# Four output blocks and four with tanh chunks of three and five; VectorE's loop end two instructions later; two tails reordered

## What is computed

```python
x = x + attention(x, mask, Wq, Wk, Wv, Wo)        # 8 batches, 512 x 1024
# then a scan over 512 time steps, carry q, p of shape (8, 1024):
def derivative(q, p, drive, coupling, bias):
    dq = q - q ** 3 / 3.0 - p + drive + jnp.tanh(q) @ coupling.T + bias
    dp = EPSILON * (q + ALPHA - BETA * p)
    return dq, dp
# classical Runge-Kutta: four derivatives a step, each at the state that
# the one before gives; then q and p are clipped to +-20
x = x + scan(rk4_step, (cond, cond), x)            # the trace of q
```

## Time and profile before

| | |
|---|---|
| median of 3 runs | 5646.72 us (5643.98 to 5647.08) |
| the profiled execution | 5647.13 us, its span 5645.3 us |
| VectorE busy | 5124.9 us, 91% of the span |
| TensorE busy, matmuls | 4394.8 us, 78% |
| ScalarE busy | 2677.3 us, 47% |
| granted TensorE clock, mean | 0.995 |
| chain that ended last | VectorE 48%, TensorE 35%, issue 13%, ScalarE 3% |

### The profile page before, as it was taken

How to read it: one execution, slowest core, us unless ns; L and a number is a source line. 1 busy time by engine, 2 the same in 40 slices (tenths; PEclk the granted TensorE clock), 3 DMA queues, 4 the chain that set the end, 5 groups by cost and what they waited for, 6 DMA issues and landing times.

```text
span 5645.3 us, 584273 instructions
## 1 busy us (share of the span) xinstructions
PE 4394.8 (78%) x263627; PEld 3697.3 (65%) x263627; DVE 5124.9 (91%) x31055; ACT 2677.3 (47%) x12552; POOL 5.7 (0%) x16
## 2 busy tenths in 40 slices
PE   7887777777777777777777777777777777777777
PEld 3436666666666666666666666666666666666666
DVE  5569999999999999999999999999999999999999
ACT  3334444444444444444444444444444444444444
POOL 0000000000000000000000000000000000000000
PEclk9999999999999999999999999999999999999999
DMA  5100000000000000000000000000000000000000
GB/s 221 47 16 0 0 7 0 7 0 0 7 0 7 0 7 0 7 0 0 7 0 7 0 7 0 0 7 0 7 0 7 0 0 7 0 7 0 7 0 7
DMA packets 11597, 57.06 MB, mean 10 GB/s; under 512 B 2616, under 2 KB 2616, under 8 KB 8512
## 3 DMA queue, kind: packets, MB, share of 16 engines
q1 hardware_dynamic: 11056, 55.84, 2.5%
q10 hardware_dynamic: 528, 1.05, 0.1%
HBM read 40.11 MB, written 16.78 MB: 10 GB/s over the span
## 4 chain that ended last, share of the span: by engine, by line
DVE 48%; PE 35%; issue 13%; ACT 3%; DVEq 0%; DMA 0%; SPq 0%; ACTq 0%
PE ps L634 30%; DVE xb L675 23%; DVE tanh_parts L675 7%; DVE xb L835 6%; ACT xb L444 3%; DVE xb L855 2%; DVE drive L675 2%; DVE xb L963 2%; DVE xb L952 2%; PE ps L523 2%; DVE xb L959 1%; DVE xb L913 1%; PE ps L541 1%; PE ps L578 1%; PE ps L557 1%
## 5 line engine op out<-in xcount | busy, mean ns | idle before, releaser
L634 PE MATMUL ps<-coup,tanh_parts 128*16 128x96 f16 (+1 forms) x262272 | 4047.0, 220 | 1171.7 <-DVE tanh_parts L675 877.6
L634 PEld LDWEIGHTS ps<-coup,tanh_parts 128*16 128x16 f16 x262272 | 3536.9, 89 | 1682.4 <-DVE tanh_parts L675 1197.8
L675 DVE SCALAR_TENSOR_TENSOR xb<-xb 128x64 f32<-128x64 f32 (+2 forms) x17413 | 3006.7, 210 | 110.5 <-issue 75.3
L444 ACT ACTIVATE xb<-xb 128x24 f32<-128x24 f32 (+1 forms) x4098 | 940.7, 230 | 2352.3 <-DVE xb L675 2276.4
L835 DVE STREAM_TRANSPOSE xb<-ps 128x96 f32<-128x96 f32 (+1 forms) x4096 | 1285.6, 314 | 38.8 <-PE ps L634 0.6
L675 DVE SCALAR_TENSOR_TENSOR tanh_parts<-xb,tanh_parts 128x24 f16<-128x24 f32 (+1 forms) x4098 | 704.3, 172 | 192.0 <-ACT xb L444 169.9
L493 ACT ACTIVATE xb<-xb 128x64 f32<-128x64 f32 x2048 | 499.6, 244 | 64.2
L450 ACT ACTIVATE tanh_parts<-xb 128x24 f16<-128x24 f32 (+1 forms) x2050 | 470.8, 230 | 64.6
L855 DVE SCALAR_TENSOR_TENSOR xb<-xb 128x64 f32<-128x64 f32 x2049 | 451.2, 220 | 0.0
L462 ACT ACTIVATE tanh_parts<-xb 128x24 f16<-128x24 f32 (+1 forms) x2048 | 356.8, 221 | 121.0
L456 ACT ACTIVATE xb<-xb 128x64 f32<-128x64 f32 x1024 | 262.6, 256 | 95.5 <-DVE xb L675 95.4
(11 more groups left out here) (69 smaller groups left out, 715.3 us busy)
## 6 DMA issues: line engine op xcount, KB each, us to landing
xb<-in_x SPq DMA_DIRECT2D x8, 2048.0 KB, 8.1
drive<-in_x_pt SPq DMA_DIRECT2D x8, 2048.0 KB, 24.5
out_pt<-drive SPq DMA_DIRECT2D x16, 1024.0 KB, 4.7
drive<-in_coupling_t SPq DMA_DIRECT2D x8, 512.0 KB, 11.6
mask_v<-in_cond SPq DMA_DIRECT2D x8, 132.0 KB
probs<-in_wo ACTq DMA_DIRECT2D x1, 1024.0 KB, 5.6
w_qkv<-in_wq SPq DMA_DIRECT2D x1, 64.0 KB, 3.7
w_qkv<-in_wk SPq DMA_DIRECT2D x1, 64.0 KB, 5.3
```

What stands on the lines that cost most here:

```text
L444: nc.scalar.activation(cols(tanh_sb, CHUNKS[j]), cols(q, CHUNKS[j]), ACT.Tanh, scale=unit_of[1.0])\
L634: last = nc.tensor.matmul(product(s, j)[SQ * g:SQ * g + ROWS, :], tanh_parts[:, s % 2, k, :], coup[:, k, part, g, n0:n1, :].rearrange("p c ...
L675: return V.scalar_tensor_tensor(out=out, in0=a, scalar=factor, in1=c, op0=ALU.mult, op1=op1)
```

## The change

`SUMS = [(0, 4), (4, 8)]` divides the outputs, in TensorE's columns, in PSUM and in the two turns. `CHUNKS` goes on dividing tanh, q 0, q 1 and the rests. On VectorE, `forecast_third` and `with_first_part` of stage 0 move from its tail into `until_rest`, so that the loop's end stands behind them. `q_sum_g0` moves from the tail of stage 3 to between q 1 and rest 1 of stage 0. `drive_step_of` moves from the tail of stage 0 to that of stage 3. Within the tails, `cubic_of(1)` goes ahead of `p_sum_g0`, and `z_of_first` ahead of `g0_of`.

```diff
 CHUNKS = [(0, 3), (3, 8)]
 NCH = len(CHUNKS)
+SUMS = [(0, 4), (4, 8)]
...
         def product(stage, j):
-            w = CHUNKS[j][1] - CHUNKS[j][0]
+            w = SUMS[j][1] - SUMS[j][0]
             return ps[:, NCH * (stage % 2) + j, 0:w * SQ]
+        def turned_rows(j):
+            return turned_sums[:, SUMS[j][0]:SUMS[j][1], :].rearrange("p c r -> p (c r)")
...
             def products(s, kj, j, begins, ends):
-                n0, n1 = CHUNKS[j]
+                n0, n1 = SUMS[j]
                 for k in range(*CHUNKS[kj]):
...
-                V.transpose(turned_sums[:, CHUNKS[j][0]:CHUNKS[j][1], :].rearrange("p c r -> p (c r)"),
-                            product(s, j)).then_inc(product_turned[j], 1)
+                V.transpose(turned_rows(j), product(s, j)).then_inc(product_turned[j], 1)
...
                 if s == 0:
                     y_less_g0()
+                    q_sum_g0()
...
                 rest_of(parity, 1, made)
-                return made
-
-            def after_rest(s, now_at, made):
-
                 if s == 0:
+
                     forecast_third(made)
                     with_first_part(1, z_first_part, z2, made)
+                return made
+
+            def after_rest(s, now_at, made):
+
+                if s == 0:
+                    cubic_of(1, made)
                     p_sum_g0()
-                    cubic_of(1, made)
-                    drive_step_of(now_at)
                     base_of(1, made)
...
                 if s == 3:
-                    g0_of(made - 1)
+                    dve.wait_ge(side_ready, made - 1)
                     z_of_first()
+                    g0_of()
                     with_first_part(0, z_first_part, z, made)
                     cubic_of(0, made)
-                    q_sum_g0()
+                    drive_step_of(1 - now_at)
                     base_of(0, made)
```

More of the change, by code:

```diff
@@ L922, in forecast_first, with g0_of @@
                 axpy(forecast[:, :], less_q[:, :], 1 / 3, q_st[3][:, :]).then_inc(forecast_ready, 1)
-            def g0_of(now):
-                dve.wait_ge(side_ready, now)
+            def g0_of():
                 axpy(g0[:, :], p_st[:, :], -BETA, q_st[0][:, :])
@@ L979, in _ @@
             for j in range(NCH):
-                last = V.transpose(turned_sums[:, CHUNKS[j][0]:CHUNKS[j][1], :].rearrange("p c r -> p (c r)"),
-                                   product(1, j))
+                last = V.transpose(turned_rows(j), product(1, j))
             last.then_inc(start_turned, 1)
@@ L988, in _ @@
             dve.wait_ge(setup, 11)
-            q_sum_g0()
+            drive_step_of(0)
             def until_rest(s, now_at, now):
@@ L1027, in until_rest @@
                 rest_of(parity, 1, made)
+                if s == 0:
+                    forecast_third(made)
+                    with_first_part(1, z_first_part, z2, made)
                 return made
@@ L1032, in after_rest @@
                 if s == 0:
-                    forecast_third(made)
-                    with_first_part(1, z_first_part, z2, made)
+                    cubic_of(1, made)
                     p_sum_g0()
-                    cubic_of(1, made)
-                    drive_step_of(now_at)
                     base_of(1, made)
```

## The result

The changed kernel takes 5701.91 us (median of 4 runs, 5699.95 to 5705.17) against 5646.9 before (4 runs): ratio 1.0099, 95% interval 1.0081 to 1.0116. It is slower, by 55 us. The forecast was 5706, range 5655 to 5750. The profiled execution has a span of 5700.3 us (before 5645.3) at the same mean granted clock, 0.995.

A forecast was written before the change was run, and what follows sets the result against it. The prediction took a ring of waits, not one engine's work, to bound the kernel. Terms -0.17 + 0.08 + 2 x 0.18 - 4 x 0.01 = +0.23 us a pass, +59 us on 5647.1: 5706, range 5655 to 5750.

The forecast's parts named there:

- The third piece on TensorE: On TensorE: matmul groups take 0.056 us; stage 3's first transpose is held 0.14 longer plus 0.04, until 1.12.
- The turns: VectorE's transposes of 128 columns take 0.24 us start to start, 0.315 long, midway between 96 and 160 columns.
- My rival, that they cost what the 96-column turn does: VectorE's 128-column transposes cost what the 96-column one does: 72 to 143 us below the sum, some 5600; chance 0.09.
- that of the 160-column one: VectorE's 128-column transposes cost what the 160-column one does: +135 us, 5841; chance 0.06.
- The loop's end: VectorE's stage 1 behind the branch: two instructions partly cover the 0.50 us gap; stage takes 2.65, gain 0.17.
- The rival of an uncovered branch: VectorE's 0.50 us gap begins only when the instruction ahead has ended: turn 0 at 1.30, +36 us, 5742; chance 0.12.
- Rest 0 just in time: On VectorE, rest 0 needn't wait for chunk 0's tanh: chain estimated at 0.47 us behind q 0, 0.48 allowed.
- the two stages 3: VectorE's stage 3, twice a pass, takes 2.70 us, a loss of 0.18 each.
- the stages 0 and 1: On VectorE, stage 0 takes 2.48 us, gain 0.01 each; stage 1 without the loop's end takes 2.61, loss 0.08.
- two stages 2: VectorE's stage 2, turn 0 at 1.05, takes 2.48 us, a gain of 0.01 each.
- The sum of +0.23: All terms for one pass of eight VectorE stages: +0.23 us, which over 256 passes is +59 us.
- The sign: Whole kernel: slower, chance 0.85; within 0.2% (11 us) 0.06; faster 0.09.

The follow-up runs named there:

- tails_alone: The changed kernel with the outputs divided three and five again, so only the loop's end and the tails differ from before: 5567.57 us.
- turns_3_5: The changed kernel, TensorE's outputs still four and four but side by side across two PSUM banks, so the turns divide three and five: 5648.43 us.
- forecast_only: The changed kernel with only `forecast_third` ahead of the loop's end and `with_first_part` behind it again: 5703.06 us.
- loop_back: The changed kernel with `forecast_third` and `with_first_part` of stage 0 behind the loop's end again, all else as changed: 5739.38 us.
- tails_loop_back: The changed kernel with outputs three and five and the loop's end again ahead of `forecast_third` and `with_first_part`: 5645.31 us.
- qpart_first: loop_back with ScalarE's `q_share` and `q_part` moved ahead of its forecast work: 5715.39 us.

## Why the prediction came out

**The third piece on TensorE: right, and the largest term.** Groups take 0.056; turn 0 comes at 1.12 in stage 3 as worked out. From tails_alone to turns_3_5 TensorE's division changes and, with it, where the outputs lie in PSUM, but not the turns' widths: +81 us. Stage 3 measured 2.68 (forecast 2.70) and stage 1 2.60 (2.61).

**The turns: the middle of the rows was right, and the size too.** From start to start 0.24, length 0.31 to 0.32. turns_3_5 prices them at 53 us, with what follows from them for rest 0. My rival, that they cost what the 96-column turn does, is out, and so is that of the 160-column one.

**The loop's end: the step that failed.** I put `cubic_of` 0.50 behind the second of the two moved instructions, at 0.75. It starts at 0.50 behind rest 1 (3003.55 less 3003.05), and the row at 0.50 in forecast_only (3005.90) and in loop_back (3002.02) confirms it from other places of the loop's end. So nothing is left of the gap (TensorE holds turn 0 until 1.12), and the stage took 2.61 where I had 2.65. I also read the cost before the change from VectorE alone. Turn 1 stood at 1.95 in the kernel before too (0.87 ahead of the 2.82 of the earlier trace rows, by its timeline), and ScalarE's `q_part` allowed no less: loop_back and tails_loop_back keep it there with a tail that is one instruction shorter. In the kernel before both paths ended within about 0.03 of each other (by its trace, ScalarE's `q_part` ended at 1.77, and VectorE's own queue would have let `z_of_third` start at 1.78, where it started at 1.80), which is why one was enough to explain the row. Taken alone, this step gave 5603 for tails_alone, which took 5568. The rival of an uncovered branch erred the same way, only further.

**Rest 0 just in time: it has to wait, and that costs 0.04.** I named this as what would make the forecast wrong, with 0.47 estimated against 0.48 allowed. From q 0 to rest 0 it is 0.47 (3004.58 to 3005.05), as estimated, but the queue would have allowed some 0.46. So rest 0 starts hardly later, yet it takes 0.18 and not 0.14, and in stage 1 it is the end of rest 0 that releases TensorE's first piece of stage 2 (its row at 3005.28 names `tanh_parts` L681). In stages 0 and 2 rest 0 waits as well, but there ScalarE's FIRST part ends later still, so it costs nothing. Stage 2 (3005.66 to 3008.18) takes 2.52 and not 2.48, with turn 0 at 1.08 and not 1.05. loop_back has both cases in one trace, with turns of 128 columns in both. VectorE, rest 1 and turn 0 of the stage 2 that follows its rest 0 at 3003.70, then the other stage 1's rest 0 with its stage 2:

```profile
3004.31 0.20 DVE L681 SCALAR_TENSOR_TENSOR tanh_parts<-xb,tanh_parts 128x40 f16<-128x40 f32 x1 [0.17 <-ACT xb L450]
...
3005.35 0.32 DVE L841 STREAM_TRANSPOSE xb<-ps 128x128 f32<-128x128 f32 x1
...
3013.93 0.18 DVE L681 SCALAR_TENSOR_TENSOR tanh_parts<-xb,tanh_parts 128x24 f16<-128x24 f32 x1
...
3014.54 0.20 DVE L681 SCALAR_TENSOR_TENSOR tanh_parts<-xb,tanh_parts 128x40 f16<-128x40 f32 x1 [0.17 <-ACT xb L450]
...
3015.63 0.32 DVE L841 STREAM_TRANSPOSE xb<-ps 128x128 f32<-128x128 f32 x1
```

and ScalarE's tanh of chunk 0 in the two stages 1:

```profile
3003.30 0.22 ACT L450 ACTIVATE xb<-xb 128x24 f32<-128x24 f32 x1
...
3013.68 0.22 ACT L450 ACTIVATE xb<-xb 128x24 f32<-128x24 f32 x1 [0.35 <-DVE xb L681]
```

In the first, tanh has ended 0.18 ahead of rest 0 (turn 1 was late there), rest 0 takes 0.14, and turn 0 comes at 1.04, as forecast. In the second, tanh ends 0.03 ahead of rest 0, rest 0 takes 0.18, and turn 0 comes at 1.09. qpart_first, which takes the first one's late turn 1 away, takes its slack away too: its rest 0 at 3011.19 is 0.18 long again, and its turn 0 at 1.08. Its expectation had this 0.04 before it ran. So the wait for tanh is shown as what costs it.

**The two errors cancelled.** For a pass: the loop's end 0.04 to 0.05 better than forecast, the two stages 3 some 0.03 in sum and the stages 0 and 1 some 0.02, against 0.08 for two stages 2. The sum of +0.23 met 0.22. The total was closer than its terms deserved, and that is luck. tails_alone shows it: there rest 0 doesn't wait, and TensorE doesn't hold turn 0 until 1.12 and so hide most of the error at the loop's end.

**The sign.** The gain and the loss are 79 and 134 us (from before to tails_alone, and from there to the changed kernel). They sit in different parts of the change: the gain in the loop's end, the loss in `SUMS`. The loss is 81 us by TensorE's division and 53 by the turns.

## What to carry to other kernels

In a ring of waits, what counts of a split is what stands ahead of the first half's signal, not the sum: equal halves added nothing to the sum of TensorE's columns or of the turns' and cost 134 us, because the first consumer waits for the first half. Where the gap at a branch is to be hidden, put the branch behind instructions whose waits are already met. If another engine's chain starts from one of them, keep that one ahead of the branch, and follow the chain to its end. And price the parts of a change separately: the better kernel, 5568 us, is this change with the outputs divided as before.

## What the hardware did that I had not expected

VectorE's gap at the loop's branch doesn't count from the instruction right before it. The next instruction started 0.50 us behind rest 1, which had to wait for tanh, with none, one or two instructions in between (kernel before and loop_back, forecast_only, changed kernel). With five in between, of which the last waits for another, turn 0 was held until 1.17. A count from the end of the last wait ahead of the branch fits all of these; only the last of them tells it from a count from rest 1, and it is one run.

A rest 0 that had to wait for ScalarE took 0.18 us, and one directly behind a turn that didn't have to took 0.14, with the same work in both (loop_back).
